# The sums T of h made by GpSimd instead of VectorE in a two-layer float16-split Strassen kernel

## What is computed

```python
# x (16, 512, 512), indices (16,) in 0..7
# W1 (512, 2048), b1, W2 (2048, 384), b2, We (8, 2048, 128), be (8, 128), all float32
h = gelu(einsum('bni,ih->bnh', x, W1) + b1)          # exact gelu
shared_x = einsum('bnh,ho->bno', h, W2) + b2
expert_x = einsum('bnh,bhp->bnp', h, We[indices]) + be[indices][:, None, :]
out = x + concatenate([shared_x, expert_x], axis=-1)
```

## Time and profile before

| | |
|---|---|
| median of three runs | 1249.43 us (1248.45 to 1249.52) |
| the profiled execution | 1250.4 us, of which the span of the instructions is 1248.5 us |
| granted TensorE clock, mean | 0.997 of 2.4 GHz |
| TensorE busy | 1236.8 us (99%) |
| VectorE busy | 940.9 us (75%) |
| ScalarE busy | 742.6 us (59%) |
| GpSimd busy | 0.2 us (0%) |
| DMA | 64.45 MB, mean 52 GB/s |

### The profile page before, as it was taken

How to read it: one execution, slowest core, us unless ns; L and a number is a source line. 1 busy time by engine, 2 the same in 40 slices (tenths; PEclk the granted TensorE clock), 3 DMA queues, 4 the chain that set the end, 5 groups by cost and what they waited for, 6 DMA issues and landing times.

```text
span 1248.5 us, 23812 instructions
## 1 busy us (share of the span) xinstructions
PE 1236.8 (99%) x9376; PEld 919.3 (74%) x9376; DVE 940.9 (75%) x1201; ACT 742.6 (59%) x944; POOL 0.2 (0%) x4
## 2 busy tenths in 40 slices
PE   8999999999999999999999999999999999999998
PEld 4446667877777777778777778777777777787775
DVE  6887658777688787787777687776887867877765
ACT  3755556556566665666656665565666656666553
POOL 0000000000000000000000000000000000000000
PEclk9999999999999999999999999999999999999999
DMA  7212323003030020201102020030200203011000
GB/s 271 100 38 90 110 68 96 7 2 102 0 101 0 8 93 0 101 0 37 64 0 101 0 67 34 0 101 0 101 0 9 92 0 101 0 42 59 1 35 35
DMA packets 25650, 64.45 MB, mean 52 GB/s; under 512 B 5136, under 2 KB 5136, under 8 KB 22416
## 3 DMA queue, kind: packets, MB, share of 16 engines
q1 hardware_dynamic: 25616, 63.99, 15.0%
HBM read 47.20 MB, written 16.78 MB: 51 GB/s over the span
## 4 chain that ended last, share of the span: by engine, by line
PE 96%; DVE 2%; DMA 1%; ACT 1%; issue 0%; SPq 0%; ACTq 0%
PE banks L1113 15%; PE banks L1114 15%; PE banks L1115 15%; PE out_ps L1115 9%; PE out_ps L1114 9%; PE out_ps L1113 9%; PE q_ps L1113 8%; PE q_ps L1114 8%; PE q_ps L1115 8%; DMA h_ring<-w_dram 1%; PE banks L1127 1%; DVE x_lo L683 0%; DVE w_lo L683 0%; PE q_ps L1127 0%; PE out_ps L1127 0%
## 5 line engine op out<-in xcount | busy, mean ns | idle before, releaser
L1113 PE MATMUL banks<-x_hi,w_hi 128*128 128x256 f16 (+1 forms) x1704 | 467.3, 274 | 4.4 <-DVE x_lo L683 2.4
L1115 PE MATMUL banks<-x_hi,w_lo 128*128 128x256 f16 (+1 forms) x1704 | 467.4, 274 | 0.0
L1114 PE MATMUL banks<-x_lo,w_hi 128*128 128x256 f16 (+1 forms) x1704 | 467.4, 274 | 0.0
L683 DVE SCALAR_TENSOR_TENSOR h_ring<-u,scale,h_ring 128x2048 f16<-128x2048 f32 x120 | 281.2, 2343 | 7.5 <-ACT h_ring L449 5.3
L516 ACT ACTIVATE kept<-banks 128x512 f32<-128x512 f32 x180 | 106.3, 591 | 167.0 <-PE banks L1115 167.0
L1113 PEld LDWEIGHTS banks<-x_hi,w_hi 128*128 128x128 f16 x1704 | 166.8, 98 | 49.9 <-issue 5.1
L1114 PEld LDWEIGHTS banks<-x_lo,w_hi 128*128 128x128 f16 x1704 | 166.8, 98 | 43.1 <-issue 0.3
L1115 PEld LDWEIGHTS banks<-x_hi,w_lo 128*128 128x128 f16 x1704 | 166.8, 98 | 21.9
L457 ACT ACTIVATE h_ring<-u,scale 128x2048 f16<-128x2048 f32 x56 | 112.1, 2002 | 96.7 <-DVE u L859 96.7
L547 ACT ACTIVATE u<-u,b_sb,undo 128x512 f32<-128x512 f32 x120 | 91.2, 807 | 121.6 <-DVE u L904 121.6
L891 DVE TENSOR_TENSOR u<-banks,kept 128x512 f32<-128x512 f32 x60 | 41.5, 692 | 157.8 <-PE banks L1115 148.8
(11 more groups left out here) (142 smaller groups left out, 1670.4 us busy)
## 6 DMA issues: line engine op xcount, KB each, us to landing
x_raw<-x_dram SPq DMA_DIRECT2D x64, 256.0 KB, 3.7
e_raw<-we_dram SPq DMA_DIRECT2D x16, 1024.0 KB, 4.7
out_dram<-x_raw SPq DMA_DIRECT2D x64, 256.0 KB, 2.4
h_ring<-w_dram SPq DMA_DIRECT2D x5, 1024.0 KB, 8.1
t_sum<-w2p_dram SPq DMA_DIRECT2D x2, 1024.0 KB, 4.8
w_sums<-w_dram SPq DMA_DIRECT2D x2, 768.0 KB, 14.6
h_ring<-w_dram SPq DMA_DIRECT2D x2, 512.0 KB, 8.1
x_raw<-w_dram SPq DMA_DIRECT2D x1, 1024.0 KB, 11.1
```

The lines of the kernel that those rows point to most:

```text
L683: return nc.vector.scalar_tensor_tensor(to, of, s, hi, ALU.mult, ALU.subtract)
L1113: nc.tensor.matmul(ps, hi, v_hi, start=start, stop=False, skip_group_check=True)
L1114: nc.tensor.matmul(ps, hi, v_lo, start=False, stop=False, skip_group_check=True)
L1115: return nc.tensor.matmul(ps, lo, v_hi, start=False, stop=stop, skip_group_check=True)
```

## The change

`add_ht` leaves VectorE's stream (five calls) and becomes a stream of its own on GpSimd, over all groups from batch PLAIN = 2 on, with the same waits and the same semaphore. GpSimd first makes a tiny subtraction of the same kind. ScalarE's conversion of T (`ht_split`) and its copy of the fifth product (`keep` with k = 2) change places in all four steps of a batch.

```diff
+        pool_warm = sb("pool_warm", [P, 3], F32)
...
+        pool_set = sem("pool_set")
...
@@ ScalarE, batch(), step 0
                 if late:
                     x_split(b, par, P3)
+                keep(b, 0, 2)
                 ht_split(b - 1, 1 - par, 3)
-                keep(b, 0, 2)
@@ step 1
+                keep(b, 1, 2)
                 ht_split(b, par, 0)
-                keep(b, 1, 2)
@@ step 2
+                keep(b, 2, 2)
                 ht_split(b, par, 1)
-                keep(b, 2, 2)
@@ step 3
+                keep(b, 3, 2)
                 ht_split(b, par, 2)
-                keep(b, 3, 2)
                 if not last:
                     x_split(b + 1, 1 - par, P6)
@@ VectorE
-            def add_ht(b, d):
...
-                add_ht(b - 1, 3)
...
-                add_ht(b, 0)
...
-                add_ht(b, 1)
...
-                add_ht(b, 2)
...
-            add_ht(B - 1, 3)
@@ GpSimd, a new block
+        @block.gpsimd
+        def _(pool):
+            def add_ht(b, d):
+
+                b11, b12, b21, b22 = (u[:, d % 2, 2 * k:2 * k + 2, NH * n:NH * (n + 1)] for k in (0, 1) for n in (0, 1))
+                base = 4 * (D * (b - PLAIN) + d)
+                pool.wait_ge(h_lo_done, D * b + d + 1)
+                nc.gpsimd.tensor_tensor(b11, b12, b11, ALU.subtract).then_inc(ht_added, 1)
+                pool.wait_ge(ht_added, base + 1)
+                nc.gpsimd.tensor_tensor(b12, b22, b12, ALU.subtract).then_inc(ht_added, 1)
+                pool.wait_ge(ht_added, base + 2)
+                nc.gpsimd.tensor_tensor(b22, b22, b11, ALU.subtract).then_inc(ht_added, 1)
+                pool.wait_ge(ht_added, base + 3)
+                nc.gpsimd.tensor_tensor(b21, b21, b22, ALU.subtract).then_inc(ht_added, 1)
+
+            nc.gpsimd.memset(pool_warm[:, :], 0.0).then_inc(pool_set, 1)
+            pool.wait_ge(pool_set, 1)
+            nc.gpsimd.tensor_tensor(pool_warm[:, 0:1], pool_warm[:, 1:2], pool_warm[:, 2:3], ALU.subtract)
+            with pool.Fori(PLAIN, B) as b:
+                for d in range(D):
+                    add_ht(b, d)
```

## The result

Over 20 runs each the median went from 1248.88 us to 1251.13 us; the ratio is 1.0016, with a 95% interval of 1.0010 to 1.0023. The medians differ by 2.3 us, the interval of the ratio stands for 1.2 to 2.9 us. That is slower, by about the 0.2% that the prediction named as what can be told, and a sixth of the 14.0 us that it forecast. The profiled execution's span is 1250.4 us (before: 1248.5 us).

The account below looks back on a forecast made before the run. TensorE, busy for 99% of the span, was taken to bound the kernel. Costs of 11.4 (step 3), 1.4 (first sums) and 1.2 us (tail) made 14.0 us on 1249.43, so 1263.4 us, range 1249.0 to 1272.0.

Parts of the forecast that it names:

- (a): Four subtractions a step removed from VectorE, 2.8 us a step: gain 0, as TensorE does not wait for VectorE there.
- (b): The four subtractions added to GpSimd: 1.22 us each, between ends of 0.69 and 1.38 us, 4.88 us for four.
- step 3: Last of a batch's four rounds of layer 1's seven products, where VectorE's sums of x run beside GpSimd's; cost 11.4 us.
- (c): GpSimd beside VectorE: they take turns, every VectorE instruction with two SBUF operands adding itself whole to the sums' time.
- (d): Step 3: GpSimd's sums end 0.88 us too late for TensorE's next first product, in 13 batches: 11.4 us.
- limit of 6.76 us: In step 3, the longest GpSimd's sums may take from their beginning before TensorE must wait for x_lo.
- (e): The other three rounds of a batch, 0, 1 and 2: cost 0, with 1.3, 0.7 and 0.5 us to spare.
- (f): The first sums, in batch 2, beside two e_lo and W2's four sums: cost 1.4 us, ends 0 and 2.8 us.
- (g): The tail, where TensorE waits for the low half of T: cost 1.2 us, ends 0 to 1.9 us.
- (h): ScalarE's copy of the fifth product ahead of the conversion: cost 0; without the swap the copy stands until 616.9.
- (i): GpSimd's warm-up subtraction and loop are hidden by 190 us in which its queue holds nothing.
- the engines do not hinder each other: Rival, 28%: sums last 4.88 us, at most 5.5, so only the tail costs: 1250.6 us, at most 1251.3.

Follow-up runs that it names:

- experiment 6: Changed kernel with VectorE's sums of x put ahead of the scales of x in step 3; 1286.68 us, ratio 1.0294 to the kernel before.
- experiment 5: Changed kernel with two more GpSimd subtractions ahead of step 3's sums: half blocks (small) 1275.8 us, ratio 1.0209; whole blocks (large) 1296.57 us, ratio 1.0360.
- experiment 2: Kernel before with only ScalarE's change of places, the sums staying on VectorE; ratio 0.9995 to the kernel before.
- experiment 3: Changed kernel with ScalarE's old order, conversion of T ahead of the copy of the fifth product; 1408.05 us, ratio 1.1266.

## Why the prediction was wrong

The direction was right and the size was not. By its own steps:

(a) VectorE's saving is worth nothing: right. (b) A GpSimd subtraction, put at 1.22 us, is 1.26 us, or 1.35 us with the handover of 0.09 us, which the estimate had left out. Four take 5.3 us instead of 4.88: this error went the other way, and with the forecast's turns it would have made step 3 lose more.

(c) That the engines take turns was right for the subtractions. **The step that failed is the price of it, in (c) and (d)**: every VectorE instruction with two operands in SBUF was to add itself whole to GpSimd's sums, 4 x 0.69 = 2.76 us in step 3. Measured is 0.73 us (6.04 against 5.31), and by the prediction's own sign (step 3's sums under 6.76 us and no gap) (c) is wrong. There are two errors. First, a meeting costs GpSimd 0.34 to 0.41 us (1.60 and 1.67 against 1.26; 0.34 us on the mean in experiment 6), not 0.69; that GpSimd's own start is hidden behind VectorE's instruction would explain the difference, and was not tried by itself, so the reason stays open. The other side pays for whole GpSimd instructions, up to 1.1 us of waiting for 0.69 us of work, and VectorE had the time. Second, the scales of x are held as well, which puts the first subtraction of x at 609.94 instead of 607.8; by then half of GpSimd's sums are done, so that two meet and not four. Either error alone is enough: two meetings at the full 0.69 us would give 5.31 + 1.38 = 6.69 us, and experiment 6, with four, gives an end 6.74 us after the low half of h (620.16 to 626.90), both just inside the limit of 6.76 us. In the changed kernel the sums end 0.6 us before it.

(d) The chain behind the sums, the limit of 6.76 us and the 13 batches were right: experiment 5 reproduced them to 0.2 us with two delays, and TensorE gave none of it back. The 11.4 us hung on the price of the meetings and their number. The sums missed the limit by 0.88 us in a forecast that had put in 2.76 us at the upper end of what no row showed; anything under 1.9 us would have cost nothing (under 1.45 us with the measured 5.31 us).

(e) Steps 0 to 2 cost nothing: right. (f) The first sums cost 0.33 us of the 1.4: P1 near 202 us is late by that, as the prediction's sign named it ("one near 202 us"). The sums ran from 189.66 to 195.62, 5.96 us and not 9.0, and were done before three of the four sums of W2 began. W2's sums, which ended 0.6 us later than before, held ScalarE's next conversion and the gelus behind it, and the gelus ended at 202.27 instead of 201.68. (g) The tail, forecast at 1.2 us, measures 1.60 us: its four sums take 5.3 us instead of 4.88, the handovers above all. Together with (f) this covers the 1.9 us by which the profiled spans differ. (h) The change of places is free, as experiment 2 shows, and the wait that the prediction named for the case without it costs 2.04 us a step, as experiment 3 shows. (i) Right.

The rival that came nearest is "the engines do not hinder each other": its time, 1250.6 us, and its main cost, the tail, are what happened, its reason is not. The engines hinder each other in every kind of step; the 0.7 us that it costs GpSimd in step 3 stays under the limit. The 60% of the forecast stood for a mechanism, which came true, and a size was tied to it that did not follow from it. That the slowdown went the forecast way is in part luck: nearly all of it is the tail's, for which the forecast had 1.2 us of its 14.0, and none of it is step 3's.

## What to carry to other kernels

Moving work to a slower engine is decided by a limit, from the end of what feeds it to the last moment at which its reader can still begin. Work that limit out for each kind of step and for the tail, where no further work covers a delay, and check what else stands in the reader's queue behind the wait: here one exchange of two lines on ScalarE was worth 155 us. Two engines that take turns need not pay alike: here the one with the short instructions waited for the whole long ones, and the one with the long instructions lost half of a short one each time.

## What the runs showed of the hardware

A small VectorE instruction with its input and output in SBUF (128x2 int32, 0.17 us) took up to 1.27 us beside a GpSimd subtraction, while scale instructions of one element (0.15 us at 645.33 and 645.51 in the changed kernel), VectorE's reductions of 2048 elements (2.27 us at 628.61) and its instructions with an input in PSUM (0.47 us at 646.50) kept their times beside one. GpSimd's handover through a semaphore to itself takes 0.09 us (1.26 to 1.35), VectorE's 0.03 us. TensorE's clock, at full speed from 190 us on in the changed kernel and in the small extra of experiment 5 with its 13 waits of 1.57 us, fell to 1.2 GHz for parts of some stretches with longer waits: in experiment 3 this is some 34 us of lost time beside 112.4 us of waits, in the large extra of experiment 5 some 8 us beside 34.5 us (estimates from the mean clock).
